# Self-attention on one core: VectorE takes the reciprocals of the softmax sums at the head of a unit, ahead of the next queries' rests

## The chip, the cores and the metric

The program runs on one core of one Trainium2 chip. The metric is the device time of one execution in microseconds; lower is better. The engines are TensorE (PE, with its weight loads as PEld), VectorE (DVE), ScalarE (ACT), GpSimd (POOL) and SyncE (SP), which here only issues transfers.

## What is computed

Two transformer blocks on x (8 batches, 512 rows, 256 columns), with a context of 64 rows of 192 columns per batch: a cross-attention block with an MLP, then a block with self-attention, cross-attention and a gated MLP. The change lies in the self-attention of the second block:

```python
def _attn(xq, xc, Wq, Wk, Wv, Wo, bo):
    q = (xq @ Wq).reshape(B, N, HEADS, D_HEAD)
    k = (xc @ Wk).reshape(B, S, HEADS, D_HEAD)
    v = (xc @ Wv).reshape(B, S, HEADS, D_HEAD)
    scale = D_HEAD ** (-0.5)
    scores = jnp.einsum('bnhd,bshd->bhns', q, k) * scale
    attn = jax.nn.softmax(scores, axis=-1)
    out = jnp.einsum('bhns,bshd->bnhd', attn, v).reshape(B, N, HEADS * D_HEAD)
    return out @ Wo + bo
...
x = _attn(_ln(x, g1, b1), _ln(x, g1, b1), Wq1, Wk1, Wv1, Wo1, bo1) + x
```

with 16 heads of 64 columns, 512 queries and 512 keys in each of 8 batches.

## The kernel before

Each engine has its own stream of instructions, written out by hand, and semaphores between them. Every engine runs one instruction after another, in the order of the code; a wait holds up all that stands behind it on its engine.

Precision: a float32 operand of a matmul is split in a rounded part ("hi") and a rest (value minus hi, "lo"), and a product is made of three matmuls (`mm3`, lines 146 to 148). The rests of large tiles are made by `dve_rest` (line 162, VectorE) and `pool_rest` (line 165, GpSimd), the rounded parts by `act_copy` (line 156) and `pool_copy` (line 159).

Self-attention is a software pipeline over "units" s = -1 ... 67, each of which holds four steps j = 0 ... 3. A pair of heads of one batch is one item; there are 64 items. In unit s the engines work on different items at once:

- item u = s + 1 is projected (queries `project(u, 0)`, keys `project(u, 1)`, values), and the largest scores of its queries are found: TensorE's `largest` (line 1419) makes scores into PSUM, VectorE's `largest` (line 1623) takes their maximum, one for each quarter q of the queries, 0 to 3; TensorE then transposes the maxima (line 152) and ScalarE writes them negated into a row that the next unit's scores subtract.
- item t = s gets its scores (TensorE, lines 1381 and 1385), its exponentials (ScalarE, line 1535, one of 128x1024 in each step) and the splitting of these exponentials: rounded parts by GpSimd in j = 0 and 3, by ScalarE in j = 1 and 2; rests by VectorE, `rests(n)`, line 162, 128x1024, both inputs in SBUF.
- item d = s - 1 gets its product with the values (`values`), and ScalarE copies the result and its row of sums out in j = 3. SP moves the sums across partitions to `SQ3` (lines 1345 and 1346).
- item d - 1 is normalised: VectorE's reciprocal of the sums (line 1650, 128x8), SP's store of it to DRAM (line 1336) and two loads that broadcast it to `RS3` (line 1340), then in GpSimd's step j = 2 the multiplication by `RS3` (line 1732, 128x512) and behind it the rounded part (line 159, 128x512) and the rest (line 165, 128x512) of the result, which TensorE's `output` takes.
- every second unit has an `output` in j = 3 (s odd), and every other one in j = 1 (s even); VectorE adds each half to x in line 1671. In every eighth unit the next batch's layer norm passes through as well.

A unit in VectorE's stream begins with the rests of the queries (line 1604, two of 64x512), which wait for ScalarE's rounded queries. Then come, before the change, the reciprocal, the rest of the last exponential of item s - 1, the rests of the keys (line 1608), of the values (line 162, 128x256), `rests(4s)` of the first exponential of item s, the additions (line 1671, here in even units), two maxima, `rests(4s + 1)`, two maxima, and `rests(4s + 2)`.

The waits of TensorE that the text comes back to, in the order of its stream (`b3_max` counts VectorE's maxima, `o3_add` its additions, `o3_lo` GpSimd's rests of the output operand):

```python
if j == 2:
    pe.wait_ge(v3_lo, u if u else -1)
    pe.wait_ge(o3_add, last_o3(s - 3) + 1)
    pe.wait_ge(b3_max, 4 * u - 1)
...
pe.wait_ge(b3_max, min(4 * u + 2, 4 * N3 - 1))
...
pe.wait_ge(o3_lo, e)
```

The first three lines stand ahead of the `largest` of quarter 1, the fifth and the last ahead of `output` in j = 3. In even units `o3_add` there is the addition of the same unit's j = 1.

Of the kernel before, what the change touches and what calls it, by code (L numbers as in the profile page):

```python
# [39 lines left out]
class Steps(Event):  # L40
# [6 lines left out]
    def next(self):  # L47
        self.n += 1
        return self.n - 1
# [53 lines left out]
def f32(ap):  # L103
    return ap.bitcast(FP)
# [6 lines left out]
def build(nc, x, ctx_in, par, con, bias, wts, out):  # L111
    es = ExitStack()
    with es:  # L113
# [28 lines left out]
        def bank(i, n=1):  # L142
            return PS[:, 512 * i:512 * (i + n)]
# [17 lines left out]
        def dve_rest(o, i, hi):  # L161
            return nc.vector.tensor_tensor(o, i, f32(hi), ALU.subtract)  # L162
# [53 lines left out]
        def xbuf(st, b):  # L216
            return XB[st][b % len(BUFS[st])]
# [32 lines left out]
        def ln_x_stats(st, b, negated=False):  # L250
            dve.wait_ge(x_in[x_at(st, b)], load_no[st, b])
            ln_stats(xbuf(st, b), C, negated)
# [7 lines left out]
        def ln_scale(k, src, n):  # L260
            dve.wait_ge(ln_rstd, k)
            dve.wait_ge(ln_nl, k - 1)
            for q in range(4):
                m = nc.vector.tensor_scalar(xt[:, q, 0:n], src[:, q, 0:n], mv[:, q, 0:1], rstd[:, q:q + 1],  # L264
                                            ALU.subtract, ALU.mult)
            m.then_inc(ln_unit.sem, 1)
# [98 lines left out]
        def dve_weight_rest(job):  # L365
            if not job.by_pool:
                dve.wait_ge(w_hi, job.number)
                dve_rest(job.lo, job.stage, job.hi).then_inc(w_lo_dve.sem, 1)
# [6 lines left out]
        def ok(v, n):  # L375
            return 0 <= v < n
# [834 lines left out]
        def after_attention0(queue):  # L1211

            queue.wait_ge(down_mm, NM - 1)
            queue.wait_ge(gelu, NM - 1)
            queue.wait_ge(w_lo_dve, [j.rest for j in g3 if not j.by_pool][-1])
            queue.wait_ge(h_lo, NM - 1)


        N3 = 8 * NB
# [72 lines left out]
        def tail3(s, j):  # L1292

            return 4 * (s - (N3 - 1)) + j - 1
# [3 lines left out]
        def after3(b):  # L1298

            return (2, b + 1) if b + 1 < NB else (3, 0)  # L1300
# [5 lines left out]
        def out3_bank(e, half):  # L1306

            return (4, 5)[half] if e == N3 - 1 else (2, 7)[half]

        def odd_bank(u):  # L1310


            return 6 if u else 0

        def v3_bank(u):
            return 6 if u else 5

        def weights3_at(s, j):

            if s == 0:  # L1320
                return g4[j:j + 1]
            return g4[2 * j + 4:2 * j + 6] if s == 1 and j < 2 else []
# [274 lines left out]
        def dve_attention1():  # L1597
            def project(u, n):
                i, src = u % 2, bank(2 + n)
                for h in range(2):  # L1600
                    hs = src[64 * h:64 * h + 64, :]
                    if n == 0:
                        dve.wait_ge(q3_hi, 2 * u + h)
                        nc.vector.tensor_tensor(qb[i][h][top, :], hs, f32(qa[i][h])[top, :], ALU.subtract  # L1604
                                                ).then_inc(q3_lo.sem, 1)
                    else:
                        dve.wait_ge(k3_hi, 2 * u + h)
                        nc.vector.tensor_tensor(ka[i][h][low, :], hs, f32(ka[i][h])[top, :], ALU.subtract
                                                ).then_inc(k3_lo.sem, 1)

            def rests(n):
                if 0 <= n < 4 * N3:
                    if n % 4 in (1, 2):
                        dve.wait_ge(p3_act, 2 * (n // 4) + n % 4 - 1)
                    else:
                        dve.wait_ge(p3_pool, 2 * (n // 4) + n % 4 // 3)
                    dve_rest(P3[1][:, n % 4, :], pst3[n % 2], P3[0][:, n % 4, :]).then_inc(p3_lo.sem, 1)

            def largest(u, q, b0):
                dve.wait_ge(b3_mm, 4 * u + q)  # L1620
                dve.wait_ge(nm3_mm, u - 1)
                dve.wait_ge(m3_set, 0)
                nc.vector.tensor_reduce(M3[:, q, 0:128:64], bank(b0, 2).rearrange("p (a b) -> p a b", a=2),  # L1623
                                        AX.X, ALU.max).then_inc(b3_max.sem, 1)

            def value(u):
                s_ = v3_s[(u // 2) % 2]
                src = bank(v3_bank(u)).rearrange("p (t a e) -> p t a e", t=2, a=2)
                tt = slice(2 * (u % 2), 2 * (u % 2) + 2)
                dve.wait_ge(v3_hi, u)  # L1630
                for c in range(2):
                    cs = slice(128 * c, 128 * c + 64)
                    m = dve_rest(s_[1][:, tt, :, cs], src[:, :, :, 64 * c:64 * c + 64], s_[0][:, tt, :, cs])
                m.then_inc(v3_lo.sem, 1)

            ahead = dve_attention2()
            for s in loop3:
                t, u, d = s, s + 1, s - 1
                b, p = divmod(max(t, 0), 8)
                more = ok(t, N3)  # L1640
                if s == 0:
                    after_attention0(dve)
                for j in range(4):
                    if ok(u, N3) and j == 0:
                        project(u, 0)
                    if ok(d - 1, N3) and j == 0:
                        k, i = (d - 1) % 2, (d - 1) // 2
                        dve.wait_ge(sum3[k], 2 * i + 1)
                        dve.wait_ge(out3[k], i - 1)
                        nc.vector.reciprocal(SR3[k], SQ3[k]).then_inc(rec3.sem, 1)  # L1650
                    if j == 0:
                        rests(4 * s - 1)
                    if ok(u, N3) and j == 0:
                        project(u, 1)
                    if s == 0 and j == 1:
                        value(0)
                    if ok(u, N3) and u > 0 and j == 1:
                        value(u)
                    if ok(u, N3) and j >= 2:
                        largest(u, 2 * j - 3, odd_bank(u))  # L1660
                    e = s - 2 if j == 3 else s - 3
                    if j in (1, 2) or j == 3 and not (ok(e, N3) and e % 2 == 1):
                        rests(4 * s + j - 1)
                    if j % 2 == 1 and ok(e, N3) and e % 2 == 1:
                        half = int(j == 1)
                        xv = xbuf(2, e // 8)[:, 2 * half:2 * half + 2, :]
                        dve.wait_ge(o3_mm, e - 1 + half)
                        dve.wait_ge(x_bias, 16 + e // 8)
                        if e % 8 > 1:
                            dve.wait_ge(o3_add, e - 3 + half)  # L1670
                        nc.vector.tensor_tensor(xv, bank(out3_bank(e, half)).rearrange("p (a c) -> p a c", a=2), xv, ALU.add
                                                ).then_inc(o3_add.sem, 1)
                        if j == 3:
                            rests(4 * s + 2)
                    if ok(u, N3) and j in (1, 2):
                        largest(u, 2 * j - 2, 2)
                    for job in weights3_at(s, j):
                        dve_weight_rest(job)
                    for _ in range(early4.get(tail3(s, j), 0)):
                        next(ahead)  # L1680
                    if more and j == 3 and p == 4:
                        ln_x_stats(*after3(b))
                    if s < 0:
                        yield s
                if more and p == 5:
                    ln_scale(18 + b, xbuf(*after3(b)), C)
            for _ in ahead:
                pass
# [430 lines left out]
        @block.vector  # L2119
        def _(e):  # L2120
            dve_products()
            attention1 = dve_attention1()
            dve_attention0(attention1)
            for _ in attention1:
                pass
# [46 lines left out]
```

## Time and profile before

| | |
|---|---|
| median of 3 runs | 2265.68 us (2265.67 to 2269.31) |
| the profiled execution | 2266.26 us, of it 2264.5 us span |
| PE, DVE, ACT, POOL busy | 93%, 71%, 66%, 47% of the span |
| granted TensorE clock in the units shown below | 1.00 |

The profile gives, for each instruction, its start and its duration, and in brackets how long its engine had been idle before it and what ended that. "L1732" is line 1732 of the kernel. Times are in microseconds from the start of the span.

### The profile page before, as it was taken

The page shows a single profiled execution, that of the slowest core. Times are in us where ns is not written, and L with a number is a line of the kernel's source. Part 1 is how long each engine was busy: PE and PEld are TensorE (multiplying, and loading weights), DVE is VectorE, ACT ScalarE, POOL GpSimd, SP SyncE. Part 2 cuts the span into 40 slices and gives each one's busy share as a digit, 9 for nine tenths or more (in the row PEclk, how much of TensorE's full clock was granted, in tenths as well). Part 3 has the DMA queues.
Part 4 walks back from the last instruction along what each step waited for, and adds up shares of the span by engine and source line. Part 5 has one row for each costly group of instructions (what it writes and reads, how often), then busy time and mean ns, then how long its engine had stood idle before and what let it go on. Part 6 is the DMA issues. An engine that isn't in the chain of part 4 may idle for free. (4 is left out here: it accounts for less than half of the span.)

```text
span 2264.5 us, 31322 instructions
## 1 busy us (share of the span) xinstructions
PE 2116.1 (93%) x11628; PEld 1768.4 (78%) x11628; DVE 1600.3 (71%) x2349; ACT 1485.3 (66%) x2157; POOL 1063.1 (47%) x830
## 2 busy tenths in 40 slices
PE   6868999998999999999999999999998799999998
PEld 4657888887778777777777777777776688998887
DVE  5576776765787777877877778777786866666553
ACT  5546888766777777777777777777774354545431
POOL 2155444431454454544544545445454666565432
PEclk8978999999999999999999999999999999999999
DMA  6810000021000100001000010010004411111000
GB/s 203 309 45 5 22 22 22 10 78 43 24 15 15 37 17 24 24 15 34 15 24 24 15 34 15 16 34 15 29 27 169 154 38 41 53 57 47 10 10 20
DMA packets 84280, 102.67 MB, mean 45 GB/s; under 512 B 29664, under 2 KB 61152, under 8 KB 83616
## 3 DMA queue, kind: packets, MB, share of 16 engines
q1 hardware_dynamic: 84128, 100.66, 13.4%
q8 instruction: 93, 1.52, 0.3%
q14 instruction: 59, 0.48, 0.1%
HBM read 65.50 MB, written 33.82 MB: 44 GB/s over the span
## 5 line engine op out<-in xcount | busy, mean ns | idle before, releaser
L146 PE MATMUL PS<-R 128*128 128x512 f32 (+1 forms) x2944 | 1021.8, 347 | 58.7 <-DVE R L162 25.7
L147 PE MATMUL PS<-R 128*128 128x512 f32 (+1 forms) x2944 | 993.6, 338 | 0.0
L148 PE MATMUL PS<-R 128*128 128x512 f32 (+1 forms) x2944 | 993.3, 337 | 0.0
L146 PEld LDWEIGHTS PS<-R 128*128 128x128 f32 x2944 | 561.7, 191 | 169.2 <-issue 36.7
L156 ACT ACTIVATE R<-PS 64x512 fp32r<-64x512 f32 (+4 forms) x860 | 459.6, 547 | 235.3 <-PE PS L1840 129.1
L148 PEld LDWEIGHTS PS<-R 128*128 128x128 f32 x2944 | 560.9, 191 | 60.6
L147 PEld LDWEIGHTS PS<-R 128*128 128x128 f32 x2944 | 562.1, 191 | 56.1
L162 DVE TENSOR_TENSOR R<-F,R 128x1024 fp32r<-128x1024 f32 (+2 forms) x418 | 462.9, 1112 | 40.0 <-POOL R L159 22.0
L159 POOL TENSOR_SCALAR R<-F 128x512 fp32r<-128x512 f32 (+1 forms) x293 | 263.4, 900 | 265.3 <-DVE F L1993 149.5
L1535 ACT ACTIVATE F<-PS 128x1024 f32<-128x1024 f32 x256 | 262.9, 1027 | 170.9 <-DVE R L162 113.3
L159 POOL TENSOR_SCALAR R<-R 64x512 fp32r<-64x512 f32 x128 | 142.5, 1127 | 390.7 <-ACT R L156 390.7
L1623 DVE TENSOR_REDUCE F<-PS 128x2 f32<-128x1024 f32 x256 | 301.5, 1216 | 6.9 <-PE PS L1419 6.9
L162 DVE TENSOR_TENSOR R<-PS,R 128x512 fp32r<-128x512 f32 (+3 forms) x348 | 181.0, 543 | 159.1 <-ACT R L156 158.5
L156 ACT ACTIVATE R<-F 128x1024 fp32r<-128x1024 f32 (+2 forms) x248 | 202.7, 831 | 61.3 <-PE PS L148 56.1
L1604 DVE TENSOR_TENSOR R<-PS,R 64x512 fp32r<-64x512 f32 x128 | 88.1, 688 | 217.5 <-ACT R L156 217.5
L165 POOL TENSOR_TENSOR R<-F,R 128x512 fp32r<-128x512 f32 (+2 forms) x124 | 226.4, 1828 | 31.7 <-ACT R L156 23.3
L156 ACT ACTIVATE F<-PS 64x512 f32<-64x512 f32 (+3 forms) x280 | 159.9, 592 | 47.7 <-PE PS L148 37.7
L1419 PE MATMUL PS<-R 128*128 128x512 f32 x512 | 163.9, 402 | 7.9 <-ACT F L156 4.9
L1385 PE MATMUL PS<-R 128*128 128x512 f32 x512 | 163.8, 401 | 7.5 <-ACT R L156 6.5
L1381 PE MATMUL PS<-R 128*128 128x512 f32 x512 | 166.8, 407 | 2.2 <-ACT R L156 1.4
L1169 POOL TENSOR_TENSOR F<-F 128x1024 f32<-128x1024 f32 x32 | 67.9, 2123 | 158.4 <-DVE F L1068 158.2
L1732 POOL TENSOR_TENSOR F<-F 128x512 f32<-128x512 f32 x64 | 82.6, 1290 | 115.2 <-DMA F<-sd 115.2
(92 smaller groups left out, 1986.9 us busy)
## 6 DMA issues: line engine op xcount, KB each, us to landing
F<-sd SPq DMA_DIRECT2D x128, 128.0 KB, 2.9
xs<-F SPq DMA_DIRECT2D x16, 512.0 KB, 2.6
F<-xs SPq DMA_DIRECT2D x16, 512.0 KB, 3.5
gd<-F SPq DMA_DIRECT2D x8, 768.0 KB, 3.9
vd<-F SPq DMA_DIRECT2D x8, 768.0 KB, 6.4
R<-gd SPq DMA_DIRECT2D x6, 1024.0 KB, 5.7
R<-vd SPq DMA_DIRECT2D x6, 1024.0 KB, 5.9
F<-in_x SPq DMA_DIRECT2D x8, 512.0 KB, 5.5
```

The source lines that it names most:

```text
L146: nc.tensor.matmul(o, L[0], Rr[0], start=start, stop=False, skip_group_check=share)
L147: nc.tensor.matmul(o, L[0], Rr[1], start=False, stop=False, skip_group_check=share)
L148: return nc.tensor.matmul(o, L[1], Rr[0], start=False, stop=stop, skip_group_check=share)
L156: return nc.scalar.activation(o, i, ACT.Identity, **k)
L159: return nc.gpsimd.tensor_scalar(o, i, 1.0, 1.0, ALU.mult, ALU.mult)
L162: return nc.vector.tensor_tensor(o, i, f32(hi), ALU.subtract)
L165: return nc.gpsimd.tensor_tensor(o, i, f32(hi), ALU.subtract)
L1381: nc.tensor.matmul(bank(h), ka[i][h][:, kk], qa[i][h], start=True, stop=False)
L1385: m = nc.tensor.matmul(bank(h), kb[i][h][:, kk], qb[i][h], start=False, stop=True)
L1419: m = nc.tensor.matmul(bank(b0 + h), qa[i][h][:, 128 * q:128 * q + 128], ka[i][h], start=True, stop=True)
L1535: nc.scalar.activation(pst3[n % 2], bank(0, 2), ACT.Exp, scale=0.125).then_inc(e3.sem, 1)
L1623: nc.vector.tensor_reduce(M3[:, q, 0:128:64], bank(b0, 2).rearrange("p (a b) -> p a b", a=2), AX.X, ALU.max).then_inc(b3_max.sem, 1)
```

## The change

In VectorE's stream of a unit, the wait for the sums of item d - 1 and their reciprocal are put ahead of the rests of the next queries. Nothing is added or removed, and the streams of the other engines stay as they are.

```diff
                 for j in range(4):
-                    if ok(u, N3) and j == 0:
-                        project(u, 0)
                     if ok(d - 1, N3) and j == 0:
                         k, i = (d - 1) % 2, (d - 1) // 2
                         dve.wait_ge(sum3[k], 2 * i + 1)
                         dve.wait_ge(out3[k], i - 1)
                         nc.vector.reciprocal(SR3[k], SQ3[k]).then_inc(rec3.sem, 1)
+                    if ok(u, N3) and j == 0:
+                        project(u, 0)
                     if j == 0:
                         rests(4 * s - 1)
```

VectorE before, from the last rest of one unit on: `q_hi` is ScalarE's rounded queries, `sum_in` the landing of the sums, `p_pool` and `p_act` the rounded exponentials, `k_hi` and `v_hi` keys and values. The third row is the one that moves.

```order
L162 TENSOR_TENSOR R<-F,R 128x1024 [waits p_act]
L1604 TENSOR_TENSOR R<-PS,R 64x512 [waits q_hi] x2
L1650 RECIPROCAL F<-F 128x8 [waits rec_out1,sum_in1]
L162 TENSOR_TENSOR R<-F,R 128x1024 [waits p_pool]
L1608 TENSOR_TENSOR R<-PS,R 64x512 [waits k_hi] x2
```

The same place in the changed kernel:

```order
L162 TENSOR_TENSOR R<-F,R 128x1024 [waits p_act]
L1648 RECIPROCAL F<-F 128x8 [waits rec_out1,sum_in1]
L1604 TENSOR_TENSOR R<-PS,R 64x512 [waits q_hi] x2
L162 TENSOR_TENSOR R<-F,R 128x1024 [waits p_pool]
L1608 TENSOR_TENSOR R<-PS,R 64x512 [waits k_hi] x2
L162 TENSOR_TENSOR R<-PS,R 128x4x64 [waits v_hi]
L162 TENSOR_TENSOR R<-PS,R 128x4x64
L162 TENSOR_TENSOR R<-F,R 128x1024 [waits p_pool]
```

The reciprocal has moved up past the two L1604; behind the queries, the rest of the last exponential now follows at once. All from there on stands in the same order.

GpSimd in the same unit is the same in both kernels. `rec_in` is the landing of the broadcast reciprocals, which hangs on the moved instruction:

```order
L159 TENSOR_SCALAR R<-R 64x512 [waits k_hi] x2
L159 TENSOR_SCALAR R<-F 128x1024 [waits d_mm,exp]
L1732 TENSOR_TENSOR F<-F 128x512 [waits d_out,rec_in1]
L159 TENSOR_SCALAR R<-F 128x512 [waits o_mul]
L165 TENSOR_TENSOR R<-F,R 128x512 [waits o_hi]
```

No instruction has moved here; the reciprocal's place on VectorE reaches this stream through `rec_in` alone.

## Rows read from the trace of the kernel before

**Rows 1.** Windows: an odd unit, then an even one; busy us (x instructions), clock, DMA.

```profile
1450.99:1468.82 17.83, 17.82 (x92) 14.61 (x91) 13.33 (x17) 13.76 (x21) 8.42 (x7) 1.00 0.05 15
1468.82:1487.32 18.50, 17.43 (x88) 14.03 (x87) 14.10 (x17) 13.73 (x21) 7.54 (x7) 1.00 0.12 44
```

**Rows 2.** Timeline, DVE: first instruction of four units; start, us, instruction, [idle before].

```profile
584.48 0.68 DVE L1604 TENSOR_TENSOR R<-PS,R 64x512 fp32r<-64x512 f32 x1 [3.36 <-ACT R L156]
...
1541.50 0.68 DVE L1604 TENSOR_TENSOR R<-PS,R 64x512 fp32r<-64x512 f32 x1 [0.53 <-ACT R L156]
...
1561.83 0.68 DVE L1604 TENSOR_TENSOR R<-PS,R 64x512 fp32r<-64x512 f32 x1 [2.19 <-ACT R L156]
...
1689.17 0.68 DVE L1604 TENSOR_TENSOR R<-PS,R 64x512 fp32r<-64x512 f32 x1 [0.54 <-ACT R L156]
```

**Rows 3.** Waits, 560 to 1740 us: us in total, times, longest us.

```profile
POOL F L1732 <- DMA F<-sd: 115.2, 63, 10.4
```

**Rows 4.** Timeline, SP: the second move of the sums, ahead of the odd unit.

```profile
1447.99 0.60 SPq L1346 DMA_DIRECT2D F<-F  x1
```

**Rows 5.** Source view of L1346: from issue to landing.

```profile
DMA to landing us min/median/max: 1.8/1.8/4.4
```

**Rows 6.** Timeline, DVE: the odd unit from 1450.99, the even one from 1468.82.

```profile
1450.99 0.68 DVE L1604 TENSOR_TENSOR R<-PS,R 64x512 fp32r<-64x512 f32 x1 [2.49 <-ACT R L156]
1453.26 0.69 DVE L1604 TENSOR_TENSOR R<-PS,R 64x512 fp32r<-64x512 f32 x1 [1.59 <-ACT R L156]
1453.88 0.19 DVE L1650 RECIPROCAL F<-F 128x8 f32<-128x8 f32 x1
1453.98 1.17 DVE L162 TENSOR_TENSOR R<-F,R 128x1024 fp32r<-128x1024 f32 x1
...
1457.53 1.22 DVE L162 TENSOR_TENSOR R<-F,R 128x1024 fp32r<-128x1024 f32 x1
...
1460.93 1.22 DVE L162 TENSOR_TENSOR R<-F,R 128x1024 fp32r<-128x1024 f32 x1
1462.06 2.35 DVE L1623 TENSOR_REDUCE F<-PS 128x2 f32<-128x1024 f32 x2
...
...
1468.82 0.68 DVE L1604 TENSOR_TENSOR R<-PS,R 64x512 fp32r<-64x512 f32 x1 [1.84 <-ACT R L156]
...
1476.49 0.68 DVE L1671 TENSOR_TENSOR F<-PS,F 128x512 f32<-128x512 f32 x1
...
1479.35 1.85 DVE L162 TENSOR_TENSOR R<-F,R 128x1024 fp32r<-128x1024 f32 x1
```

**Rows 7.** Timeline, POOL in the odd unit.

```profile
1456.19 1.04 POOL L159 TENSOR_SCALAR R<-F 128x1024 fp32r<-128x1024 f32 x1
1458.94 1.29 POOL L1732 TENSOR_TENSOR F<-F 128x512 f32<-128x512 f32 x1 [1.72 <-DMA F<-sd]
1460.32 0.62 POOL L159 TENSOR_SCALAR R<-F 128x512 fp32r<-128x512 f32 x1
1461.02 2.27 POOL L165 TENSOR_TENSOR R<-F,R 128x512 fp32r<-128x512 f32 x1
```

**Rows 8.** Timeline, POOL and DVE: two places where both want SBUF at once.

```profile
1201.16 0.62 POOL L159 TENSOR_SCALAR R<-F 128x512 fp32r<-128x512 f32 x1
1201.33 1.52 DVE L162 TENSOR_TENSOR R<-F,R 128x1024 fp32r<-128x1024 f32 x1
...
1294.03 1.29 POOL L1732 TENSOR_TENSOR F<-F 128x512 f32<-128x512 f32 x1 [3.77 <-DMA F<-sd]
1294.55 1.85 DVE L162 TENSOR_TENSOR R<-F,R 128x1024 fp32r<-128x1024 f32 x1
```

**Rows 9.** Timeline, PEld: before `output` (odd unit), before quarter 1 (even unit).

```profile
1463.40 0.19 PEld L146 LDWEIGHTS PS<-R 128*128 128x128 f32 x1 [0.41 <-DVE F L1623]
...
1477.29 0.30 PEld L1419 LDWEIGHTS PS<-R 128*128 128x128 f32 x2 [0.38 <-issue]
```

**Rows 10.** Timeline, ACT: the copies of sums and outputs, even unit.

```profile
1482.59 2.27 ACT L156 ACTIVATE F<-PS 1x512 f32<-1x512 f32 x4 [0.27 <-PE PS L148]
```

## The prediction

> **What bounds the kernel now.** I read the windows of two neighbouring units first. In the odd one TensorE is busy 17.82 of 17.83 us, at a granted clock of 1.00: no other engine's time can be shortened to any use there, but whatever makes TensorE wait is added to the unit. In the even one TensorE is busy 17.43 of 18.50 us and idle for 1.07 [rows 1]. Next, the length of the stage: from the first instruction of the unit at 584.48 to that of the unit at 1689.17 there are 60 units in 1104.7 us, a mean of 18.41 [rows 2]. Every eighth unit, with the layer norm, takes 20.33 us (1541.50 to 1561.83) [rows 2].
>
> Then the waits: GpSimd's multiplication L1732 stood 115.2 us, in 63 places, waiting for the broadcast reciprocals [rows 3]. That is the wait which the change can shorten. Last, the timelines of the two units, to see who stands behind whom.
>
> In the odd unit TensorE's `output` is released by two engines at once. VectorE's maximum of quarter 2, the first of the pair at 1462.06 (2.35 for both, 0.08 of it overlapped), ends at about 1463.28 [rows 6]; GpSimd's L165 ends at 1461.02 + 2.27 = 1463.29 [rows 7]; TensorE's weight load goes at 1463.40 [rows 9]. By rows 1 there is no slack there. In the even unit the weight load of quarter 1 at 1477.29 had idled for 0.38 us; the profile names no releaser ("issue"), but L1671 ended at 1476.49 + 0.68 = 1477.17, which is the same 0.12 before it as 1463.28 is before 1463.40, and the code waits there for just this addition [rows 6, 9]. TensorE's matmuls of before still ran then, so this too has no slack to speak of. ScalarE's first copy of the outputs starts when TensorE ends its product with the values [rows 10], and the copies run back to back into the next unit; a late TensorE in the even unit is thus a late next unit.
>
> **The change, step by step.**
>
> *The reciprocal finds room.* Ahead of the odd unit the sums are moved at 1447.99 and land 1.8 us later, at 1449.8 [rows 4, 5]. VectorE is free from 1448.50 on and idles 2.49 us until the queries come at 1450.99; ahead of the even unit it idles 1.84 [rows 6]. The reciprocal of 0.19 us fits in this idle time, and its new wait costs nothing as long as the move lands within 1450.99 - 1447.99 = 3.0 us. Behind the waiting instruction stand the queries' rests, and behind those all of VectorE.
>
> *VectorE gains a little.* At the old place, L1604 ended at 1453.95 and the rest behind the reciprocal at 1455.15, 1.20 later. Where a rest stands directly behind another instruction, it starts about 0.08 before that one's end (as the reciprocal does at 1453.88, L1604 ending at 1453.95) and takes 1.22, so it ends 1.14 later. Gain: 0.06 us for everything behind it [rows 6]. ScalarE's next exponential waits for this rest, so it too comes 0.06 earlier.
>
> *The multiplication comes early.* From the reciprocal at 1453.88 to L1732 at 1458.94 there are 5.06 us of store, broadcast and landing [rows 6, 7]. With the reciprocal at about 1449.8 the landing is at 1454.9. GpSimd is free for it only at 1456.19 + 1.04 = 1457.23 [rows 7], 6.24 us after the unit's start. Even a reciprocal just ahead of the queries, at 1450.8, would land in time, at 1455.9; the even unit has the same order and so the same margin. So the DMA wait disappears altogether, and L1732 starts when the copy before it ends. That copy hangs on the keys' copies, which VectorE's rest delays, so it gains the same 0.06: L1732 starts at about 1457.16 and ends at 1458.46.
>
> *There it meets `rests(4s)`.* This is the cost. VectorE starts `rests(4s)` at 1457.53 [rows 6], with the gain at 1457.47; GpSimd is 0.3 us ahead. What happens then, two places show. At 1294.03 L1732 had started 0.52 ahead of a rest; the rest took 1.85 instead of 1.22 and ended at 1296.40, 1.08 after L1732's end at 1295.32. At 1201.16 a GpSimd copy was only 0.17 ahead and ended at 1201.78; the rest ended at 1202.85, 1.07 after it [rows 8]. The engine that comes second waits for the whole of the first one's instruction. The other way round, the rest at 1460.93 came 0.09 before L165 and kept its 1.22, while L165 took 2.27 [rows 6, 7]. So `rests(4s)` will end at 1458.46 + 1.07 = 1459.53 instead of 1458.75: between 0.75 and 0.80 later, and I take **0.77**. The Trainium skill has this rule (SBUF — State Buffer, "Who interferes with whom"): a VectorE instruction with two SBUF inputs and a GpSimd instruction that reads SBUF exclude each other, and issue order decides who blocks; the rows agree, and it speaks against this change. The skill also says (Perfetto Trace Analysis, "GPSIMD Engine Instruction") that a GpSimd span in a profile is not to be trusted and the start-to-start spacing is better; from 1458.94 to 1460.32 that is 1.38 instead of 1.29, which would make the loss 0.09 larger a unit and the time 5.5 us longer; the rests that ended 1.07 or 1.08 after the reported end speak for the reported one.
>
> *Where it lands, odd units.* VectorE runs without a gap from `rests(4s)` through the maxima, so quarter 2's maximum ends 0.77 later, at about 1464.05. GpSimd's L165 comes out of the way (multiplication, copy behind the rest, L165: done by about 1461.4, before `rests(4s + 1)` starts at 1460.93 + 0.77 = 1461.70), but it was only one of two releasers. TensorE's `output` goes 0.75 to 0.77 later, and TensorE is dense from there on: **+0.77**.
>
> *Even units.* L1671 stands behind `rests(4s)`, so it ends at 1477.94, and TensorE's quarter 1 with all behind it is 0.77 late; the product with the values, ScalarE's copies and the next queries follow. In return `rests(4s + 1)`, now blocked by L165 (1.85 instead of 1.22 [rows 6]), becomes free. That saves 0.63, but on a branch (maxima, transposes) which then is no longer the last. **+0.77** against the undisturbed 18.50, and the layer-norm units, which are even ones with a longer tail, alike.
>
> *What is given back.* The 60 units are 30 odd, 22 even, 7 with layer norm and the short first one of 17.2 us: 30 x 17.83 + 22 x 18.50 + 7 x 20.33 + 17.2 = 1101.4 us if each took the length of those shown [rows 1, 2]. They took 1104.7, because late broadcasts push L1732 about. With the landing 2 us ahead of need this 3.3 us should go.
>
> **Sum.** 61 units have both a multiplication and `rests(4s)` with projections around: 61 x 0.77 = 47.0; less 3.3; +43.7 us. The profiled execution took 2266.3, the median of the runs is 0.6 less: 2265.7 + 43.7 = 2309.4, rounded to **2310**. Bounds from the same rows: a delay of 0.63 (what L1732's block cost the rest at 1294.55) gives 61 x 0.63 - 3.3 = +35; 0.85 (GpSimd gains no 0.06 and starts at 1457.23, so 1458.52 + 1.07 = 1459.59 against 1458.75) gives 61 x 0.85 - 3.3 = +49. So the likeliest case alone runs from 2300 to 2315.
>
> **The rivals.**
>
> *A. The order turns (7%).* If L1732 starts only after `rests(4s)` has begun (something of 0.35 us in the new path: the start of a GpSimd instruction whose wait has long ended is not in the rows), the rest is not delayed and L1732 is held until 1458.7. It then ends at about 1459.9, the copy at 1460.6, and L165 runs from 1460.7, just ahead of `rests(4s + 1)` at 1460.87. The loss of about 0.85 moves there: it costs in the 30 odd units, while in the even ones the maxima are late no more than now. 30 x 0.8 - 3.3 = +21: 2287.
>
> *B. Slack takes it (4%).* If TensorE's wait in the odd units is more GpSimd's than VectorE's, and the even units absorb the late L1671 in their 1.07 us of idle time: only the maximum before the transposes would count, 30 x 0.3 - 3 = +6: 2272. Against it speaks the 0.12 us spacing in both weight loads.
>
> *C. Faster (5%).* L1732 and the rest do not block each other at this place, or with less than 0.1 us. Then the odd units gain 0.06, L165 no longer strikes `rests(4s + 1)`, and the 3.3 us of late broadcasts go: 2265.7 - 3.3 - 3.7 = 2259. It decides if L1732 loses its lead and its length both; rows 8 speak against it twice.
>
> *D. The new wait holds up the queries (3%).* If the sums land more than 3.0 us after their issue, the queries' rests wait: each microsecond is one for the unit. The longest landing was 4.4, the median 1.8 [rows 5]. Half a microsecond in half of the units on top: 2325.
>
> *E. No change (3%).* The two effects of C and a partly hidden block cancel: 2261 to 2270.
>
> **Chances and range.** The likeliest case has 78%. A, B and D are slower too, so slower has 78 + 7 + 4 + 3 = 92%, faster by over 0.2% (4.5 us, about what a measurement of this kernel can tell from no change) 5%, within it 3%. The range reaches from A to a little beyond the upper bound: 2284 to 2318, which leaves out B, C, D and E, 15%, and a few per cent of the likeliest.
>
> **What would show it.** In the profile of the changed kernel: the reciprocal in VectorE's idle time before L1604, with L1604 still released by ScalarE; L1732's wait for the DMA near zero, down from 115.2 us; `rests(4s)`, the second 128x1024 rest behind L1604, at about 1.9 to 2.0 us instead of 1.22, and `rests(4s + 1)` of even units at 1.22 instead of 1.85; odd units of about 18.6 and even ones of about 19.3 us; new idle time of TensorE ahead of `output`, of quarter 1 and of quarter 2, released by VectorE. The prediction is wrong if `rests(4s)` keeps its 1.22, or if it is longer and the units are not.

## The result and the profile after

The changed kernel takes 2315.48 us in the median of 4 runs (2314.78 to 2319.58), the kernel before 2265.68 in the median of 4 (2264.93 to 2269.31): a ratio of 1.021, with a 95% interval of 1.0198 to 1.0222. It is 49.8 us slower; forecast were 44. The time lies inside the forecast range of 2284 to 2318, just above what the likeliest case alone allowed (2300 to 2315).

The profiled execution has a span of 2313.0 us, 48.5 more. An odd and an even unit in the windows view (columns as in [rows 1]):

```profile
1490.99:1509.52 18.53, 18.05 (x92) 14.58 (x91) 14.30 (x16) 13.79 (x21) 8.24 (x7) 1.00 0.05 15
1509.52:1528.84 19.32, 17.48 (x88) 14.04 (x87) 14.23 (x17) 13.78 (x21) 9.42 (x7) 1.00 0.12 42
```

The odd unit went from 17.83 to 18.53 us, the even one from 18.50 to 19.32, and TensorE's idle time from 0.01 to 0.48 and from 1.07 to 1.84. VectorE's timeline shows what it did in them:

```profile
1493.28 0.69 DVE L1604 TENSOR_TENSOR R<-PS,R 64x512 fp32r<-64x512 f32 x1 [1.60 <-ACT R L156]
1493.89 1.21 DVE L162 TENSOR_TENSOR R<-F,R 128x1024 fp32r<-128x1024 f32 x1
...
1497.48 2.05 DVE L162 TENSOR_TENSOR R<-F,R 128x1024 fp32r<-128x1024 f32 x1
...
1501.72 1.21 DVE L162 TENSOR_TENSOR R<-F,R 128x1024 fp32r<-128x1024 f32 x1
1502.85 2.34 DVE L1623 TENSOR_REDUCE F<-PS 128x2 f32<-128x1024 f32 x2
...
1507.78 0.20 DVE L1648 RECIPROCAL F<-F 128x8 f32<-128x8 f32 x1
1509.52 0.68 DVE L1604 TENSOR_TENSOR R<-PS,R 64x512 fp32r<-64x512 f32 x1 [1.54 <-ACT R L156]
...
1516.00 2.07 DVE L162 TENSOR_TENSOR R<-F,R 128x1024 fp32r<-128x1024 f32 x1
1517.99 0.68 DVE L1671 TENSOR_TENSOR F<-PS,F 128x512 f32<-128x512 f32 x1
...
1520.85 1.21 DVE L162 TENSOR_TENSOR R<-F,R 128x1024 fp32r<-128x1024 f32 x1
```

The reciprocal now stands in the idle time before L1604, which ScalarE still releases: its wait holds nothing up. The second large rest, `rests(4s)`, takes 2.05 and 2.07 us instead of 1.22. The rest of the even unit that had taken 1.85, `rests(4s + 1)`, is down to 1.21, what rests take in [rows 6] where GpSimd is not in the way. GpSimd, in its own timeline:

```profile
1496.14 1.04 POOL L159 TENSOR_SCALAR R<-F 128x1024 fp32r<-128x1024 f32 x1
1497.16 1.29 POOL L1732 TENSOR_TENSOR F<-F 128x512 f32<-128x512 f32 x1
1498.54 1.48 POOL L159 TENSOR_SCALAR R<-F 128x512 fp32r<-128x512 f32 x1
1500.10 1.29 POOL L165 TENSOR_TENSOR R<-F,R 128x512 fp32r<-128x512 f32 x1
```

L1732 has no bracket any more: it starts where the copy before it ends, at 1497.16, 1.78 earlier in its unit than in [rows 7], and ends at 1498.45. The rest that VectorE had started at 1497.48 ends at 1499.53, 1.08 behind. The short copy after it takes 1.48 instead of 0.62 and ends behind that rest, at 1500.02: now GpSimd is the later one.

Three places where TensorE's weight loads had to wait, and below them the two of TensorE's matmuls that hang on the first and the third:

```profile
1500.72 0.30 PEld L1419 LDWEIGHTS PS<-R 128*128 128x128 f32 x2 [0.90 <-DVE F L1623]
1504.12 0.19 PEld L146 LDWEIGHTS PS<-R 128*128 128x128 f32 x1 [0.35 <-DVE F L1623]
1518.78 0.30 PEld L1419 LDWEIGHTS PS<-R 128*128 128x128 f32 x2 [1.16 <-issue]
```

```profile
1500.72 0.73 PE L1419 MATMUL PS<-R 128*128 128x512 f32 x2 [0.48 <-DVE F L1623]
1518.81 0.70 PE L1419 MATMUL PS<-R 128*128 128x512 f32 x2 [0.77 <-DVE F L1671]
```

In the odd unit TensorE waits for the maxima of VectorE: ahead of the `largest` of quarter 2 for the maximum of quarter 0, where all of its 0.48 us of idle time stands, and at `output`, where its weight load had waited before as well (0.41, now 0.35). In the even unit it waits for L1671, which ends at 1518.67. And the waits of the whole stage, 560 to 1790 us because it ends some 50 us later than in [rows 3]:

```profile
POOL F L1732 <- DMA F<-sd: 17.5, 3, 12.1
```

Of 115.2 us of waiting for the broadcast in 63 places 17.5 us in 3 are left, and 15.7 of them stand behind the 61 units, where the pipeline runs empty. The change did what it says; the time was lost behind it.

The wait that is left inside them is an experiment that the changed kernel makes by itself. In the even unit that starts at 1701.40 the broadcast came late, and L1732 started behind the whole rest, as GpSimd's timeline and VectorE's show:

```profile
1709.33 1.29 POOL L1732 TENSOR_TENSOR F<-F 128x512 f32<-128x512 f32 x1 [1.75 <-DMA F<-sd]
```

```profile
1707.87 1.22 DVE L162 TENSOR_TENSOR R<-F,R 128x1024 fp32r<-128x1024 f32 x1
```

There `rests(4s)` kept its 1.22 us and the unit took 18.48, where the other 21 even units took 19.28 to 19.32.

### The profile page after: what moved, and what is told of

It is laid out like the page before. It is cut to its first block and busy times, and to the rows that moved or that the text cites. A ratio compares the mean times of both kernels' runs of the same rounds, so it can differ in the third digit from the quotient of the medians.

```text
span 2313.0 us, 31322 instructions
## 1 busy us (share of the span) xinstructions
PE 2123.6 (92%) x11628; PEld 1767.6 (76%) x11628; DVE 1640.2 (71%) x2349; ACT 1487.2 (64%) x2157; POOL 1098.0 (47%) x830
## 5 line engine op out<-in xcount | busy, mean ns | idle before, releaser
L146 PEld LDWEIGHTS PS<-R 128*128 128x128 f32 x2944 | 562.0, 191 | 168.3 <-issue 36.3
L148 PEld LDWEIGHTS PS<-R 128*128 128x128 f32 x2944 | 561.4, 191 | 60.6
L147 PEld LDWEIGHTS PS<-R 128*128 128x128 f32 x2944 | 562.6, 191 | 56.1
L162 DVE TENSOR_TENSOR R<-F,R 128x1024 fp32r<-128x1024 f32 (+2 forms) x418 | 498.5, 1197 | 38.5 <-POOL R L159 21.6
L159 POOL TENSOR_SCALAR R<-F 128x512 fp32r<-128x512 f32 (+1 forms) x293 | 334.8, 1144 | 398.5 <-PE PS L148 192.8
L1604 DVE TENSOR_TENSOR R<-PS,R 64x512 fp32r<-64x512 f32 x128 | 88.0, 688 | 177.8 <-ACT R L156 177.8
L165 POOL TENSOR_TENSOR R<-F,R 128x512 fp32r<-128x512 f32 (+2 forms) x124 | 195.5, 1579 | 32.1 <-ACT R L156 23.7
L1419 PEld LDWEIGHTS PS<-R 128*128 128x128 f32 x512 | 88.0, 188 | 94.7 <-DVE F L1623 38.7
```

The lines of the kernel that those rows point to most:

```text
L146: nc.tensor.matmul(o, L[0], Rr[0], start=start, stop=False, skip_group_check=share)
L147: nc.tensor.matmul(o, L[0], Rr[1], start=False, stop=False, skip_group_check=share)
L148: return nc.tensor.matmul(o, L[1], Rr[0], start=False, stop=stop, skip_group_check=share)
L159: return nc.gpsimd.tensor_scalar(o, i, 1.0, 1.0, ALU.mult, ALU.mult)
L165: return nc.gpsimd.tensor_tensor(o, i, f32(hi), ALU.subtract)
L1419: m = nc.tensor.matmul(bank(b0 + h), qa[i][h][:, 128 * q:128 * q + 128], ka[i][h], start=True, stop=True)
```

## The experiments

The leading theory: L1732, freed of its wait, takes SBUF ahead of VectorE's `rests(4s)` and stops it until it is through. The rival: the reciprocal's new place on VectorE, or its transfers at another time, cost the time. All kernels below have the changed kernel as base, unless said otherwise. An added or removed line moves the numbers behind it, so the multiplication is L1731 in one of them and L1734 in others.

**The product alone, early.** The kernel before, with

```diff
-                        pool.wait_ge(in3[f % 2], 2 * (f // 2) + 1)
                         pool.wait_ge(d3_out, f)
-                        nc.gpsimd.tensor_tensor(OA, OA, RS3, ALU.mult).then_inc(mul3.sem, 1)
+                        nc.gpsimd.tensor_tensor(OA, OA, OA, ALU.mult).then_inc(mul3.sem, 1)
```

> The order of the kernel before, with the reciprocal behind the queries' rests. L1732 multiplies OA by itself instead of by RS3 and does not wait for the broadcast, so that it starts as soon as GpSimd is free; the softmax is left unnormalised (the transfers are still made). Theory 1, L1732 too early takes SBUF from rests(4s): rests(4s) near 2.05 us, odd units 18.6, even 19.3 to 19.4, time 2316 to 2320 (the changed kernel's 2315.5 and 61 x 0.06 of lost gain). Theory 2, the reciprocal's new place on VectorE or the earlier transfers cost the time: 2266 or less.

2299.36 us (2 runs), ratio 1.0142 (1.0117 to 1.0166). Most of the loss is there with the reciprocal in its old place, so the rival falls. It is 17 us less than I expected, and the timelines of GpSimd and VectorE say why:

```profile
1484.02 1.03 POOL L1731 TENSOR_TENSOR F<-F 128x512 f32<-128x512 f32 x1
...
1484.36 1.78 DVE L162 TENSOR_TENSOR R<-F,R 128x1024 fp32r<-128x1024 f32 x1
```

A product of a tile with itself takes 1.03 us, not 1.29, and the rest ends 1.09 behind it: 1.78 instead of 2.05. The odd units take 18.31, 0.48 over the undisturbed 17.83. The product of a tile with itself gives a wrong result; only the time is used. The experiment was meant to remove one suspect and became a second size of the other.

**Half a product.**

```diff
-                        nc.gpsimd.tensor_tensor(OA, OA, RS3, ALU.mult).then_inc(mul3.sem, 1)
+                        nc.gpsimd.tensor_tensor(OA[:, 0:256], OA[:, 0:256], RS3[:, 0:256], ALU.mult).then_inc(mul3.sem, 1)
```

> The changed kernel, with L1732 on the first 256 of 512 columns of OA only; the other half of the result stays unnormalised. Theory 1: L1732 lasts 0.65 us and ends at about 6.80 in the unit, rests(4s) ends 1.07 later at 7.87 instead of 8.52: 0.11 over the kernel before instead of 0.77. 61 x 0.11 - 3.3, and some 8 us for the eight units with the layer norm's root ahead of L1732: about 2277 (2270 to 2282). Theory 2: nothing changes, 2312 to 2316.

2273.01 us (8 runs), ratio 1.003 (1.0019 to 1.0041). L1732 lasts 0.74 us, the rest 1.50:

```profile
1462.63 0.74 POOL L1732 TENSOR_TENSOR F<-F 128x256 f32<-128x256 f32 x1
...
1462.96 1.50 DVE L162 TENSOR_TENSOR R<-F,R 128x1024 fp32r<-128x1024 f32 x1
```

With 1.29, 1.03 and 0.74 us of GpSimd's instruction, `rests(4s)` takes 2.05, 1.78 and 1.50, and the kernel 2315, 2299 and 2273: the loss follows the length of this one instruction. (The middle one has the reciprocal in its old place, which by the prediction's 0.06 us a unit is worth some 4 us.)

**The product behind the rest.**

```diff
                         pool.wait_ge(d3_out, f)
+                        if ok(t, N3):
+                            pool.wait_ge(p3_lo, 4 * t)
```

> The changed kernel, with L1732 waiting for rests(4s) of the same unit. Theory 1: rests(4s) is back at 1.22 us in all units, also in those with the layer norm's root. L1732 runs from 7.8 to 9.1, and L165 comes within 0.1 us of the start of rests(4s + 1) in odd units. If VectorE comes first, 2259 to 2263; if GpSimd does, the block moves to rests(4s + 1) and the 30 odd units pay 0.8 to 0.9: about 2286. Theory 2: 2312 to 2316.

2260.26 us (10 runs), ratio 0.9973 (0.996 to 0.9986). One wait on GpSimd turns the loss of 49.8 us into a gain of 6: the early reciprocal itself costs nothing. Odd units take 17.75, even ones 18.48. The case that was open, who comes first at `rests(4s + 1)` of odd units, went to VectorE by 0.07 us:

```profile
1454.53 1.22 DVE L162 TENSOR_TENSOR R<-F,R 128x1024 fp32r<-128x1024 f32 x1
...
1454.60 2.29 POOL L165 TENSOR_TENSOR R<-F,R 128x512 fp32r<-128x512 f32 x1
```

That is a narrow place. Had L165 been 0.2 us earlier, the rest would have paid, by an estimate from the kernel before: in the two units where L165 started 0.09 us ahead of `rests(4s + 1)`, at 629.93 and 1662.89, the rest took 2.29.

**The layer norm's root later.**

```diff
-                    if more and j == 0 and p == 5:
+                    if more and j == 3 and p == 5:
                         ln_pool_rstd(18 + b)
```

> The changed kernel, with GpSimd's root of the layer norm (L258) in step 3 of its unit instead of step 0, behind L1732. Theory 1 with L258 as part of the block: the eight units with the root (19.50 us in the changed kernel, rests(4s) 3.03 us) become like other odd units, 18.52 with rests(4s) 2.05: about 8 us less, 2307 to 2309. If these units are longer for another reason: 2314 to 2317.

2307.94 us (4 runs), ratio 1.0178 (1.0161 to 1.0195), 7.5 less than the changed kernel. The eight units with the root take 18.50 and their `rests(4s)` 2.04 us, like all odd ones. The loss in these units, 1.67 us each, was more than twice that of the other odd units (0.64 in the mean), and the root's place next to L1732 made the difference.

**The wait in one parity only.**

```diff
                         pool.wait_ge(d3_out, f)
+                        if ok(t, N3) and s % 2 == 0:
+                            pool.wait_ge(p3_lo, 4 * t)
```

and the same with `s % 2 == 1`.

> The changed kernel, with L1732 waiting for rests(4s) in even units only; in odd ones it starts early as in the change. Theory 1 with a cost in either parity: odd units stay at 18.52 (22 of them) and 19.50 (8, with the layer norm's root), even ones return to 18.49 and 20.27: 2260 and 22 x 0.77 + 8 x 1.77 = 2291. If only the even units' addition L1671 matters, 2260 to 2265.

> The same wait in odd units only. Theory 1: odd units 17.75, even ones 19.30 and 21.10: 2260 and 29 or 30 x 0.82 = 2284. If the even units' idle time of TensorE (1.07 us) absorbed the block, 2260 to 2265, and e5 would hold all of the loss.

2289.15 us (2 runs, ratio 1.0098, 1.0077 to 1.0119) with the wait in even units, 2283.76 (2 runs, 1.0075, 1.0046 to 1.0103) with it in odd ones. First instructions of an odd unit, of the even one behind it and of the next odd one, in the run with the wait in odd units:

```profile
1469.11 0.68 DVE L1604 TENSOR_TENSOR R<-PS,R 64x512 fp32r<-64x512 f32 x1 [0.99 <-ACT R L156]
...
1486.86 0.68 DVE L1604 TENSOR_TENSOR R<-PS,R 64x512 fp32r<-64x512 f32 x1 [1.54 <-ACT R L156]
...
1506.17 0.68 DVE L1604 TENSOR_TENSOR R<-PS,R 64x512 fp32r<-64x512 f32 x1 [1.01 <-ACT R L156]
```

17.75 and 19.31 us: the odd unit is healed, the even one keeps all of its loss. In the other run it is 18.49 and 18.47. Both parities pay in full, and the two losses, 28.9 and 23.5 us over 2260.26, add up to 52.4 of the 55.2 between the changed kernel and the one with the wait everywhere. The two runs with the wait in odd units lie 10 us apart (2278.76 and 2288.75), so the 23.5 is rough. The profiled executions say it better: over the 60 units, by the starts of L1604, the losses are 30.2 and 24.6 us, of 54.9 in the changed kernel. The rival B of the prediction, slack in the even units, falls with it.

**The wait in the kernel before.** The same two lines as in the third experiment, but with the reciprocal in its old place.

> The kernel before, with the same wait of L1732 for rests(4s). There the broadcast lands at about 7.9 in the unit, behind the end of rests(4s) at 7.76, so the wait should be idle: 2264 to 2268. Should this be as fast as the changed kernel with the wait (2260), the gain there comes from the wait, and not from the reciprocal's place.

2268.46 us (10 runs), ratio 1.0012 (0.9999 to 1.0024): no difference. GpSimd still waits for the broadcast instead:

```profile
POOL F L1734 <- DMA F<-sd: 116.6, 63, 9.9
```

So the 6 us of the third experiment come from the reciprocal's new place with its early landing, and not from the wait. The wait only makes it usable. The result, 2260.26, is close to what the prediction's rival C gave for a kernel in which the two instructions do not strike each other (2259).

**A second wait.** To the third experiment is added, ahead of L165,

```diff
                         pool.wait_ge(o3_hi, f)
+                        if ok(u, N3):
+                            pool.wait_ge(b3_max, 4 * u + 1)
```

> The changed kernel with L1732 waiting for rests(4s) as before, and L165 waiting for the maximum of quarter 1 as well, so that it comes just behind the start of rests(4s + 1) in both parities. rests(4s + 1) of even units falls from 1.85 to 1.22, the idle time before the transposes from 0.93 to 0.3. If ScalarE's row of copies bounds the even units, nothing else moves: 2258 to 2261, the same as with one wait. If VectorE's maxima bound them, 29 x 0.5 less: about 2245.

2258.85 us (5 runs), ratio 0.9963 (0.9951 to 0.9976), with one wait 0.9973 (0.996 to 0.9986): the two are not told apart. In the even units `rests(4s + 1)` is at 1.22 us, and TensorE's idle time has only moved, as its timeline shows; ScalarE's stands below it:

```profile
1477.67 0.66 PE L152 MATMUL PS<-F 128*128 128x128 f32 x4 [0.33 <-DVE F L1623]
1480.90 0.73 PE L1385 MATMUL PS<-R 128*128 128x512 f32 x2 [0.73 <-ACT R L156]
```

```profile
1477.37 2.27 ACT L156 ACTIVATE F<-PS 1x512 f32<-1x512 f32 x4 [0.78 <-PE PS L148]
1479.67 2.40 ACT L156 ACTIVATE R<-PS 1x512 fp32r<-1x512 f32 x4
1482.09 1.03 ACT L1535 ACTIVATE F<-PS 128x1024 f32<-128x1024 f32 x1
```

0.93 us before the transposes and 0.14 before the scores in the third experiment have become 0.33 and 0.73, and the unit takes 18.43. The first of ScalarE's eight copies waits for TensorE's product with the values, and they run back to back into the next unit: this row, and not the maxima, sets the even unit's length, as the first of the two cases expected above has it. Both versions beat the kernel before and the changed one.

## Why the prediction was right

The direction, the mechanism and the place came out as written, and the size within 6 us. The size owes its place in the range to the margin above the likeliest case: the excess has a cause that the prediction did not have (the units with the root, below).

*The reciprocal finds room*: yes. It stands in the idle time of all 61 units and ends 0.42 to 1.56 us before the queries come, and L1604 waits for ScalarE as before. Rival D had no unit.

*VectorE gains 0.06*: yes. The rest behind L1604 starts at 2.89 in the unit, lasts 1.21 and so ends at 4.10 instead of 4.16, and the third experiment's odd units are 0.08 shorter than those shown of before.

*The multiplication comes early*: yes, but the margin was smaller than I put it. In the odd unit shown, the sums were moved at 1487.99, the store went out at 1490.03 and the broadcasts at 1493.01, 2.98 us behind the store, where [rows 6, 7] had suggested one fixed 5.06 us for store and broadcast together. GpSimd was free at 1497.16; it was enough all the same.

*The block of 0.77*: `rests(4s)` grew by 0.83, less the 0.06 gained, which is 0.77. In 59 of the 60 units the rest ended 1.07 to 1.10 us behind L1732's reported end; the other is the one with the late broadcast. The reported end was the right one to reckon with: from the start-to-start spacing, 1.38 us, the rest of the odd unit would have taken 2.14 and not 2.05. The Trainium skill (Perfetto Trace Analysis, "GPSIMD Engine Instruction") prefers that spacing; here the reported end held. That the time did come out 5.5 us above 2310, just what the prediction reckoned for the spacing, is a coincidence: the excess lies in eight units, not in all. The prediction's sign for this step, 1.9 to 2.0 us for `rests(4s)`, was a slip against its own sum, in which the rest runs from 1457.47 to 1459.53, 2.06 us.

*Where it lands*: the two odd units shown differ by 0.70 instead of 0.77; the weight load of `output` now follows the maximum by 0.06 us where it had followed both its releasers by 0.12. TensorE is held up in them one step earlier than the working has it, ahead of quarter 2, a wait that the kernel before did not have there; the prediction has it among its signs, but reckoned the odd units by `output` alone. In the unit, its weight load goes 0.79 later than in the kernel before (there at 1459.93) and that of `output` 0.72 later, so either place gives about the same loss. The even units shown differ by 0.82, layer-norm units by 0.77 (21.10 against 20.33).

*What is given back*: yes; the odd units without the root all lie between 18.51 and 18.55, where they had been spread from 17.78 to 18.49.

The term that was mis-sized is "61 x 0.77", for it took the eight units with the layer norm's root for units like the others. Over the 60 units from 586.28 to 1739.39 the sum is, by the starts of L1604: 22 odd ones at +0.64 in the mean (14.1 us), 8 with the root at +1.67 (13.3), 22 even ones at +0.67 (14.8), 7 with layer norm at +0.77 (5.4), and 0.8 for the first: 48.4 us. The root's units were reckoned at 6.2 and cost 13.3, and the experiment that moved the root gives those 7 us back (7.5). All others together cost 35.1, where 52 x 0.77 less the 3.3 given back makes 36.7, which took a little off the miss. The timelines of a unit with the root in the changed kernel, GpSimd's and VectorE's:

```profile
1572.82 1.01 POOL L258 TENSOR_TENSOR F<-F 128x4 f32<-128x4 f32 x1
1573.82 1.28 POOL L1732 TENSOR_TENSOR F<-F 128x512 f32<-128x512 f32 x1
```

```profile
1573.15 3.03 DVE L162 TENSOR_TENSOR R<-F,R 128x1024 fp32r<-128x1024 f32 x1
```

The rest starts 0.67 us before L1732's reported start, and yet waits for its end at 1575.10 and ends 1.08 behind that. In the kernel before, the same root ran beside the same rest, which took its 1.22; there L1732 came later. By the rule of the prediction, read from the reported starts, VectorE should have won. That rule holds in the 51 other units in which the two meet, and fails in these eight. The Trainium skill (SBUF — State Buffer, "SBUF: two separate sides") gives the shared way to SBUF to whichever of the two instructions starts first. By the reported starts the trace agrees in those 51 units and not in the eight; whether GpSimd took it before its reported start, no run here shows.

## What to carry to other kernels

A wait that costs its own engine nothing can be what keeps two engines apart. Before an instruction on GpSimd is made earlier, look at what VectorE runs in the new place: if it reads two SBUF tiles there, as the rests here do, the later of the two can lose the whole of the other's remaining time. Where an early transfer is wanted but the early use is not, move the transfer and hold the use with a wait on the instruction that it must not strike. And shortening an instruction gains nothing where what stands behind it has another, later releaser, as with the second wait.

## What the runs showed of the hardware that was not expected

- In the eight units with a 128x4 power on GpSimd directly ahead of L1732, the order of the reported starts did not decide. With the whole product (1.28 us) the rest took 3.03. In the same place the product of the tile with itself took 1.84 instead of 1.03 and the rest 1.61, and half a product 1.25 instead of 0.74 and the rest 1.32, so there mostly the product waited. With the third experiment's wait the rest of these units takes 1.22, and with the root moved away 2.04, as in other odd units. Whether GpSimd claims its way to SBUF for the next instruction while the power still runs was not settled; only that the power's neighbourhood is needed for it is shown. Nor did the power block: it started some 0.33 us ahead of the rest in the kernel before, and the rest took 1.22.
- A GpSimd product of a 128x512 float32 tile with itself took 1.03 us, one of two tiles 1.29.
- TensorE busy for 17.82 of 17.83 us was no floor: with the wait of the third experiment the same unit took 17.75, and TensorE was busy for 17.75 of it.
- One unit near the start of the stage, which the change does not touch, is 1.2 us longer in the changed kernel's profile (19.25 against 18.03). Its mean granted clock is 0.91 in both. In the changed kernel the stretch at the lower level (0.50, 1.2 GHz) lies at 563.5 to 566, where TensorE is busy throughout; it had done nothing from 560 to 562 and then worked for a microsecond at 1.00; in the kernel before the clock is 0.50 at 556 to 558 and 1.00 from 562 on. That the place of the stretch makes the 1.2 us is likely, and was not tested. It does not make the result: of the 48.5 us by which the spans differ, 48.4 lie in the 60 units behind it.
